# Router weights as the stationary operand, four token blocks on four column strips, and one transposition of the logits

## The reference

```python
x = x + tanh(g_xattn) * xattn(ctx_1024, layernorm(x), ...)   # 128 x 64 x 128, 8 heads of 128
x = x + tanh(g_ffn) * ffn(layernorm(x), ...)

def ffn(x, Wr, br, W1, b1, W2, b2):          # 8192 tokens, width H = 128, E = 8 experts, K = 2
    logits = einsum('bsh,he->bse', x, Wr) + br
    probs = softmax(logits)
    top_p, top_i = top_k(probs, 2)
    cw = sum(one_hot(top_i, E) * top_p[..., None], axis=-2)
    h = relu(einsum('bsh,ehd->bsed', x, W1) + b1)
    y = einsum('bsed,edh->bseh', h, W2) + b2
    return einsum('bseh,bse->bsh', y, cw)
```

## Time and profile before

| | |
|---|---|
| median of 3 runs | 797.5 us (796.06 to 798.2) |
| span of the profiled execution, first to last instruction | 795.7 us |
| granted TensorE clock, mean | 0.993 |
| TensorE busy | 760.7 us, 96% |
| VectorE, ScalarE, GpSimd busy | 528.3, 496.9, 446.1 us |

### The profile page before, as it was taken

One profiled execution on the slowest core, in us unless ns is written; L12 is line 12 of the kernel. 1 busy time (PEld: TensorE's weight loads), 2 busy tenths in 40 slices (PEclk: granted clock), 3 DMA queues, 4 the chain that ended last, 5 costly groups with the idle time before them and its releaser, 6 DMA issues.

```text
span 795.7 us, 17460 instructions
## 1 busy us (share of the span) xinstructions
PE 760.7 (96%) x5392; PEld 643.6 (81%) x5392; DVE 528.3 (66%) x1829; ACT 496.9 (62%) x1630; POOL 446.1 (56%) x455
## 2 busy tenths in 40 slices
PE   7999999999999999999999999999999999979788
PEld 6778777777888988778988878898877888868765
DVE  5636677685857567677658776776868567565536
ACT  3677777676766566766656667565567665554522
POOL 2233264646552544785655586665568566556664
PEclk9999999999999999999999999999999999999999
DMA  7735151542454642174754226664414555634523
GB/s 198 209 150 194 60 213 69 211 146 81 145 188 154 205 153 72 38 231 143 237 189 143 65 76 218 206 212 163 127 54 140 180 191 188 212 112 116 154 77 87
DMA packets 119791, 119.42 MB, mean 150 GB/s; under 512 B 14585, under 2 KB 94994, under 8 KB 119698
## 3 DMA queue, kind: packets, MB, share of 16 engines
q1 hardware_dynamic: 111088, 102.41, 39.1%
q0 software_dynamic: 7680, 15.74, 6.8%
q10 hardware_dynamic: 930, 0.15, 0.1%
HBM read 35.94 MB, written 41.55 MB: 97 GB/s over the span
## 4 chain that ended last, share of the span: by engine, by line
PE 77%; issue 6%; POOL 6%; DVE 5%; ACT 4%; DMA 1%; another core or an unknown queue 1%; SPq 1%; POOLq 0%; ACTq 0%; DVEq 0%
PE shared L1426 13%; PE batch L1364 11%; PE batch L1377 11%; PE hid_ps L1294 8%; PE xy_ps L1308 7%; PE batch L1372 6%; PE shared L1217 3%; PE shared L1219 3%; PE shared L1218 3%; ACT probs L746 3%; PE batch L1308 2%; POOL probs L676 2%; PE xy_ps L1271 2%; POOL yg L666 2%; PE batch L1354 2%
## 5 line engine op out<-in xcount | busy, mean ns | idle before, releaser
L676 POOL TENSOR_TENSOR probs<-probs,rsums 128x512 f32<-128x512 f32 x128 | 132.9, 1039 | 231.7 <-DVE rsums L1147 230.1
L746 ACT ACTIVATE probs<-batch,neg_max 128x128 f32<-128x128 f32 x512 | 180.5, 374 | 2.0 <-DVE neg_max L1151 2.0
L651 POOL DMA_INDIRECT sorted_x<-xn,row_of x120 | 124.4, 1036 | 33.6 <-issue 28.7
L827 ACT ACTIVATE qT<-shared,tb 128x512 f32<-128x512 f32 x128 | 87.2, 696 | 85.6 <-PE shared L1219 72.4
L1377 PE MATMUL batch<-pT_sb,kvn 128*128 128x512 f32 x256 | 133.7, 604 | 2.9 <-ACT pT_sb L754 2.9
L1364 PE MATMUL batch<-kvT,qT 128*128 128x128 f32 x1024 | 135.4, 275 | 0.8 <-ACT qT L827 0.8
L1426 PE MATMUL shared<-M,oT 128*128 128x128 f32 x1024 | 125.5, 276 | 0.3
L1364 PEld LDWEIGHTS batch<-kvT,qT 128*128 128x128 f32 x1024 | 124.4, 192 | 1.2 <-ACT qT L827 1.2
L1426 PEld LDWEIGHTS shared<-M,oT 128*128 128x128 f32 x1024 | 119.4, 192 | 1.6 <-issue 1.6
L746 ACT ACTIVATION_READ_ACCUMULATOR probs<-batch,neg_max 128x1 f32 x512 | 110.2, 215 | 0.0
L1147 DVE RECIPROCAL rsums<-sums 128x4 f32<-128x4 f32 x128 | 22.7, 178 | 130.4 <-ACT probs L746 119.9
(11 more groups left out here) (168 smaller groups left out, 1243.4 us busy)
## 6 DMA issues: line engine op xcount, KB each, us to landing
wt<-wall SPq DMA_DIRECT2D x124, 321.0 KB
sorted_x<-yg SPq DMA_DIRECT2D x36, 512.0 KB, 4.8
xt<-sorted_x SPq DMA_DIRECT2D x162, 64.0 KB
sorted_y<-y_sb SPq DMA_DIRECT2D x78, 128.0 KB
kv<-in_ctx_dram SPq DMA_DIRECT2D x16, 256.0 KB
kv<-in_x_dram SPq DMA_DIRECT2D x16, 256.0 KB
xres<-in_x_dram SPq DMA_DIRECT2D x32, 128.0 KB
out_dram<-x SPq DMA_DIRECT2D x15, 256.0 KB
```

What stands on the lines that cost most here:

```text
L651: nc.gpsimd.indirect_dma_start(xs[k % SETS][:, :], bass.IndirectOffsetOnAxis(ap=row_of[:, g, choice, c:c + 1], axis=0), xn[:, g % 2, c, :] ...
L676: nc.gpsimd.tensor_tensor(pv, pv, rsums[:, m % 2, :].unsqueeze(2).broadcast_to([P, 4, P]), ALU.mult).then_inc(probs_ready, 1)
L746: last = nc.scalar.activation(probs[:, m % 2, c * P:(c + 1) * P], batch_ps[m % BANKS][:, c * P:(c + 1) * P], ACT.Exp, bias=neg_max[:, m % ...
L827: nc.scalar.activation(qT[:, g % 2, :, number, :], sh[:, :].rearrange("p (b i) -> p b i", b=GB), ACT.Identity, bias=tb[:, number:number + ...
```

## The change

The router's weights `Wr_f` become 128 x 32, with 24 columns of zeros, and they are the stationary operand now. Each of the four blocks of `xT` is the moving operand of a product whose 32 rows of output go to another strip of 32 partitions of the bank. ScalarE copies the 128 x 128 result to `logitT`, and a new use of the shared banks, "turn_logits", transposes it, so that VectorE reads the logits as before, with a stride of 32.

In `SHARED` the router moves from place "a" of slot 5 to place "c" of slot 4, "turn_logits" takes its place, query 2 moves from slot 4 to slot 5, and query 4 from slot 5 to slot 6, which has two queries after.

```diff
-    4: [("project", 0, 0, "a"), ("turn_x", -1, 0, "b"), ("query", 1, 2, "c")],
-    5: [("router", -1, 0, "a"), ("query", 1, 3, "b"), ("query", 1, 4, "c")],
-    6: [("project", 0, 1, "a"), ("query", 1, 5, "b")],
+    4: [("project", 0, 0, "a"), ("turn_x", -1, 0, "b"), ("router", -1, 0, "c")],
+    5: [("turn_logits", -1, 0, "a"), ("query", 1, 2, "b"), ("query", 1, 3, "c")],
+    6: [("project", 0, 1, "a"), ("query", 1, 4, "b"), ("query", 1, 5, "c")],
...
-        Wr_f = sb("Wr_f", [P, E])
+        Wr_f = sb("Wr_f", [P, 32])
+        logitT = sb("logitT", [P, P])
...
+            nc.gpsimd.memset(Wr_f[:, :], 0.0).then_inc(const_step, 1)
...
-            act.dma_start(Wr_f[:, :], Wr).then_inc(got_gates, 16)
+            act.wait_ge(const_step, 20)
+            act.dma_start(Wr_f[:, 0:E], Wr).then_inc(got_gates, 16)
...
+                elif what == "router":
+                    wait_shared(act, shared_full, "turn_logits", g - 1, 0)
+                    nc.scalar.activation(logitT[:, :], sh[:, 0:P], ACT.Copy).then_inc(shared_out[bank], 1)
...
-                    nc.vector.tensor_tensor(logit[:, :, :], shared[bank][:, 0:4 * E].rearrange("p (c e) -> p c e", c=4),
+                    nc.vector.tensor_tensor(logit[:, :, :], shared[bank][:, 0:P].rearrange("p (c e) -> p c e", c=4)[:, :, 0:E],
...
-                    pe.wait_ge(const_step, 19)
+                    pe.wait_ge(const_step, 20)
...
                         for c in range(4):
-                            last = nc.tensor.matmul(sh[:, c * E:(c + 1) * E], xT[:, c * P:(c + 1) * P], Wr_f[:, :], start=True, stop=True)
+                            last = nc.tensor.matmul(sh[32 * c:32 * c + 32, 0:P], Wr_f[:, :], xT[:, c * P:(c + 1) * P], start=True, stop=True)
+                    elif what == "turn_logits":
+                        wait_shared(pe, shared_out, "router", g, 0)
+                        last = nc.tensor.transpose(sh[:, 0:P], logitT[:, :], ident[:, :])
```

More of the change, by code:

```diff
@@ L458, in shared_at @@
         def shared_at(n, place, reader):
-            on_dve = ("project", "router", "place", "table")
+            on_dve = ("project", "turn_logits", "place", "table")
             return [(what, g, number, bank) for what, g, number, places, bank, _ in uses[n]
@@ L968, in aggregate_kv @@
                     if g == 0:
-                        dve.wait_ge(const_step, 19)
+                        dve.wait_ge(const_step, 20)
                     dve.wait_ge(stats_done, 2 * (g + 1))
@@ L980, in read_logits @@
                 if s == 5 and 0 <= g < G:
-                    bank, _ = use_at["router", g, 0]
-                    wait_shared(dve, shared_full, "router", g, 0)
-                    nc.vector.tensor_tensor(logit[:, :, :], shared[bank][:, 0:4 * E].rearrange("p (c e) -> p c e", c=4),
+                    bank, _ = use_at["turn_logits", g, 0]
+                    wait_shared(dve, shared_full, "turn_logits", g, 0)
+                    nc.vector.tensor_tensor(logit[:, :, :], shared[bank][:, 0:P].rearrange("p (c e) -> p c e", c=4)[:, :, 0:E],
                                             br_all[:, :].unsqueeze(1).broadcast_to([P, 4, E]), ALU.add).then_inc(shared_out[bank], 1)
-                    wait_shared(dve, shared_out, "router", g, 0)
+                    wait_shared(dve, shared_out, "turn_logits", g, 0)
                     nc.vector.tensor_reduce(top[:, :], logit[:, :, :], AX, ALU.max).then_inc(route_step, 1)
```

## The result

The changed kernel takes 798.9 us (median of 10 runs, 798.6 to 801.24) where the kernel before takes 797.19 us (10 runs, 796.06 to 798.45). The ratio over all the runs is 1.0032 (that of the two medians would be 1.0021), with a 95% interval of 1.0023 to 1.0042: slower by 1.8 to 3.3 us, about 2.5. The forecast was +5.3 us, 802.8 us. The sign is as forecast; the change is half as large.

The account below looks back on a forecast made before the run. TensorE, busy 96% of the span, was taken to bound the kernel. Bare periods at 1.74 + 7s and full ones at 9s - 3.6 gave 16s - 1.8, +5.3 us with s = 0.44: 802.8 us, range 796.5 to 810.

Parts of the forecast that it names:

- point 2: The new router's eight narrow instructions on TensorE: s + 0.30 us in each group.
- the term s: Time from the new router's first start to its last: 0.44 us taken, ends 0.11 and 0.77.
- the middle: New router's strips overlap in a staggered way, 0.44 us from first to last start; chance 0.40.
- a rival at 0.12: Full overlap of the router's four strips: 0.11 us from first to last start, 797.5 us, no change; chance 0.12.
- Point 2, entry and exit: TensorE going to the router's narrow form and back: 0.10 + 0.09 us.
- Points 1, 3 and 4: Old router goes, -0.81 us; transposition +0.11 us a group, its wait hidden; wait for the `xT` copy hidden by 0.06 us.
- Point 5: ScalarE's shorter copy in bare periods: slot 5's product earlier by 0.93 - s, or about 1.09 - s in four.
- Point 6: Moved queries in bare periods: +0.70 us in slot 6, a new wait of 0.57 us in slot 7; 8.9 us in all.
- The sum: Bare periods 1.74 + 7s, full periods 9s - 3.6, total 16s - 1.8 us: +5.3 us.
- Theory A: Formed after the result: the loss is ScalarE's order in bare periods, the query at slot 6's place "c" and its wait.
- Theory B: Formed after the result: the loss is the router's new form, its entry and exit, or something outside the slots.

Follow-up runs that it names:

- Experiment 5: The changed kernel with the router's four products run twice in the same order: 788.16 us, ratio 1.0068 to the kernel before.
- Experiment 4: The changed kernel with all four products on one strip, logits copied as 32 x 512 and turned by four small transpositions: 816.43 us, ratio 1.0241 to the kernel before.
- experiment 1: The kernel before with its old router, only the queries moved as in the changed kernel: 798.19 us, ratio 0.9999.
- experiment 3: The changed kernel with query 2 in slot 3 instead, queries 3 and 4 in slot 5, query 5 in slot 6: 800.49 us, ratio 1.0040 to the kernel before.
- experiment 8: The changed kernel with order and router of before in bare periods, so changed in full periods only: 780.25 us, ratio 0.9974 to the kernel before.
- experiment 9: The kernel before with the change in bare periods and those without a router, full periods as before: 802.83 us, ratio 1.0054.
- experiment 7: The changed kernel with `Wr_f` and `logitT` allocated last, all other buffers lying as before: 784.28 us, ratio 1.0032 to the kernel before.
- experiment 2: The kernel before with its old router, query 2 moved from slot 4 to place "c" of slot 3: 796.26 us, ratio 0.9986.
- experiment 6: The kernel before with 608 unused bytes a partition, so that later buffers lie as in the changed kernel: 783.56 us, ratio 1.0011.
- experiment 10: The kernel of experiment 8 with query 2 in slot 3 in the bare periods of groups 0 to 3: 795.08 us, ratio 0.9958 to the kernel before.
- experiment 11: The kernel of experiment 8 with the bare period of group 3 changed as well: 798.15 us, ratio 0.9999 to the kernel before.

## Why the prediction was half right

**The step that failed is point 2, the term s.** I took 0.44 us, "the middle", on the thought that starts stay in order and each next product's first instruction has to wait for the second one of the product before. Measured is 0.16 us: four instructions start at once, one on each strip, and the other four 0.13 us later. The term was 16 s, so this alone is 16 x (0.16 - 0.44) = -4.5 us. Experiment 5 shows what is true in its place: the four strips run side by side and no pair queues behind another; only a product's own two instructions follow one another (+0.22 us for a second set). Experiment 4 shows that nothing but the strips does it (1.00 us against 0.36).

The Trainium skill, TensorEngine Tiling (Array Packing), section Tiling Modes, had said that tiles on different strips load and multiply in parallel. I had it in the prediction as a rival at 0.12, and the trace agrees with it, with its 0.36 us. The rows for one strip, couldn't speak for or against it, and my middle value was a choice between two ends, not a reading. The rule should have had the weight.

**Point 2, entry and exit,** was right: 0.10 us in. To get out takes what is left of 0.36 less s, 0.20 us, of which 0.11 is the usual pace. Experiment 4's small transpositions show the entry again: L1370's last start there is 119.22 + 1.06 - 0.28 = 120.00, and the first of them starts 0.21 us later.

**Points 1, 3 and 4** came as read. In full periods 0.57 us stand in place of 0.81, a gain of 0.24, and the slots show 0.21. The transposition costs 0.11 us and waits for nothing. In group 3 the router waits for VectorE's x as the query did before, 0.74 us.

**Point 5, slot 5 of bare periods.** With s = 0.16 it gives a gain of 0.93 - 0.16 = 0.77 us; slots 4 and 5 gain 0.24 + 0.47 = 0.71. In groups 3, 6, 9 and 12 slots 4 to 7 come to 0.38 by slot where 1.27 - 0.93 = 0.34 was worked out. The mechanism, ScalarE's constant chain from the last pass of place "c" to the product, holds.

**Point 6, slot 7's wait,** was right to 0.01 us: 0.57 forecast, 0.58 found, and +0.70 in slot 6. Experiments 1 and 3 show that the query's place makes it: the wait is there with the old router, and it goes when the query goes.

**The sum.** The sum's constant, 1.74 - 3.6, is -1.86 and was written as -1.8. With the measured s the formula gives 16 x 0.16 - 1.86 = +0.7 us. The rest up to about +2.2 by the trace: the bare periods cost 3.2 us in place of 1.74 + 7 x 0.16 = 2.9; full periods gain 1.5 us in place of 3.6 - 9 x 0.16 = 2.2, since group 14's loses 0.1 and group 15's gains at most 0.1, which I had counted as full ones; and the first tile's wait, 0.49. The first two are terms mis-sized, by 0.3 and 0.7 us. The third is a step that was not in the sum at all. These errors have the other sign than that of s: they made good a part of its 4.5 us, so that the total missed by 2.8. That it missed by no more is luck.

**Theory A** holds in part. The loss is in the bare periods: experiments 8 and 9 take the change apart into -2.0 and +4.3 us. But that slot 7's wait is the cause of it is too much said: experiment 1 has the same wait and costs nothing. In a bare period of groups 0 to 2 the wait and the query in slot 6 together cost what slots 4 and 5 give back, 1.27 us; what is left over is the router itself, at a place where TensorE is waited for. In group 3 the same move of the queries gains 0.95 us with the old router, and the changed kernel loses 0.38: there the new router at place "c" also brings back the wait for VectorE's `x1`, 0.74 us. Theory B's entry and exit are real, 0.2 us a group, but they are within the 0.57 us that beats the old router's 0.81 wherever TensorE bounds.

**Open:** why the first tile's weights come 0.5 to 1 us late. The wait appears in six kernels that have changed bare periods ahead of the first tile (the changed one, and experiments 3, 4, 5, 7 and 9), and in none of the others (1, 2, 6, 8, 10, 11). Where the buffers lie is ruled out by experiments 6 and 7, group 3's period alone by experiment 11. SyncE's rows with `wall`, the sorted weights, ahead of the tile, of the kernel before and then of the changed one (each row is two issues):

```profile
211.36 1.23 SPq L556 DMA_DIRECT2D wt<-wall  x2
214.19 1.14 SPq L556 DMA_DIRECT2D wt<-wall  x2
```

```profile
212.53 1.23 SPq L557 DMA_DIRECT2D wt<-wall  x2
215.63 1.83 SPq L557 DMA_DIRECT2D wt<-wall  x2
```

The first pair keeps its place against the slots: it is 1.17 us later, and the slots there are 1.18 us later too. But in the second pair one issue takes 1.19 us where each took 0.50. It is so in all thirteen traces: of these four issues each takes 0.50 to 0.56 us in the seven kernels without the wait, and one takes 0.95 to 1.32 us in each of the six with it. What goes with it is a 16 KB packet of instructions in DMA queue q8, 1.1 to 1.4 us long: in the six it is under way when the long issue begins, in the seven it starts after all four issues are over. The changed order has one instruction more on TensorE and one more on ScalarE in each group, so such a packet could well come earlier against the slots. That it is what makes the weights late is not shown: no run moved that packet alone.

## What to carry to other kernels

Sum a change by kind of period, not by the mean over the kernel: this one gains 0.2 us in each of seven periods and loses 0.4 to 0.6 in each of seven others, and taking only the first half of it made the kernel faster (ratio 0.9974; with the early query, 0.9958; but 0.9999 with group 3's period changed as well, of which the slots explain a part). Before moving work on the busiest engine, ask of its old place whether it lay in the shadow of another engine's in-order work: what lies there is free, and half the work at a place where that other engine waits for it is dearer. Where two ends of a price lie far apart and a rule speaks for one, the middle is no safe value. Compare starts slot by slot afterwards, since a disturbance of 1 us at the start of one trace is as large as half of this result.

## What the runs showed of the hardware

Four float32 products, each two instructions and each on its own strip of 32 columns, took TensorE 0.36 us from the first start to the next line: one instruction of each product started at once, within 0.02 us, and the other four 0.13 us later. On one strip it was 1.00 us, in steps of 0.11. A second set on the same strips added 0.22 us. Going from full-width work to narrow work cost 0.10 us, and back 0.09, here as at L1319. ScalarE's copy of 128 x 128 held it for 0.17 us from start to start, though each took 0.28. The granted clock of a stretch at the start of the kernel, 12 to 17 us, was 0.66 in one execution and 1.00 in another, and all that followed was 0.95 us apart. In six kernels one issue of weights by SyncE took 0.95 to 1.32 us in place of 0.50 to 0.56, each time while a 16 KB packet of instructions was under way, and TensorE waited for the weights.
